# Reordering the first loads, the first basis blocks and four PSUM copies of a graph-network kernel

## The reference, cut to what matters

```python
h = jnp.maximum(_layernorm(x, axis=-1), 0.0)
x = x + _L0_gnn_ref(h, edge_index, Wq, Wk, Wv, bq, bk, bv)
# layer 0: q, k, v = proj(Wq), proj(Wk), proj(Wv); only the last head has scores that are not all zero
masked = jnp.zeros_like(scores).at[-1, src, dst].set(scores[-1, src, dst])
att = jax.nn.softmax(masked, axis=-1)
out = jnp.einsum('hnm,hmd->hnd', att, v)
# layer 1, twice, for r in range(2):
w = jnp.einsum('rb,bio->rio', att, basis)      # 30 matrices of 512 x 512, two sums of them
msg = jnp.where((edge_type == 0)[:, None], msgs[0], msgs[1])
agg = jax.ops.segment_sum(msg, row, num_segments=x.shape[0]) + x @ root + bias
```

## Time and profile before

| what | value |
|---|---|
| median of 3 runs | 642.83 us (642.61 to 643.83) |
| the profiled execution, own time | 641.3 us |
| its span in the trace | 639.5 us |
| TensorE busy | 592.7 us, 93% of the span |
| VectorE busy | 489.5 us, 77% |
| ScalarE busy | 229.5 us, 36% |
| GpSimd busy | 183.9 us, 29% |
| mean DMA rate | 192 GB/s |

### The profile page before, as it was taken

One profiled execution on the slowest core, in us unless ns is written; L12 is line 12 of the kernel. 1 busy time (PEld: TensorE's weight loads), 2 busy tenths in 40 slices (PEclk: granted clock), 3 DMA queues, 4 the chain that ended last, 5 costly groups with the idle time before them and its releaser, 6 DMA issues.

```text
span 639.5 us, 6502 instructions
## 1 busy us (share of the span) xinstructions
PE 592.7 (93%) x2062; PEld 326.1 (51%) x2062; DVE 489.5 (77%) x1054; ACT 229.5 (36%) x455; POOL 183.9 (29%) x229
## 2 busy tenths in 40 slices
PE   4899999998899999999988999997988889999997
PEld 2444445653346644334765786443545445555544
DVE  5489999999999998374747666464687778898266
ACT  2001121510002310206710673310767677785111
POOL 7920000001100000003620372075756556730000
PEclk9899999999998999999999989999989999999999
DMA  8957657669987597700600013475766667740000
GB/s 299 408 198 299 239 191 252 272 237 420 420 333 279 189 377 271 331 1 0 262 3 0 2 38 121 176 216 172 216 184 218 193 208 212 239 142 1 0 16 34
DMA packets 27737, 122.64 MB, mean 192 GB/s; under 512 B 4528, under 2 KB 9392, under 8 KB 22704
## 3 DMA queue, kind: packets, MB, share of 16 engines
q1 hardware_dynamic: 15376, 64.46, 26.9%
q0 software_dynamic: 12320, 57.68, 26.4%
HBM read 120.56 MB, written 1.57 MB: 191 GB/s over the span
## 4 chain that ended last, share of the span: by engine, by line
PE 79%; DVE 10%; DMA 3%; issue 3%; ACT 2%; another core or an unknown queue 2%; POOL 1%; SPq 0%; DVEq 0%
PE ps L1353 25%; PE ps L1696 12%; PE ps L1405 12%; PE ps L1736 8%; PE ps L1589 7%; PE ps L1801 4%; DMA mixm<-basis_p_dram 3%; PE ps L1382 2%; PE ps L1492 2%; DVE node L953 2%; PE ps L1791 2%; DVE mixm L871 2%; DVE node L949 1%; PE ps L1360 1%
## 5 line engine op out<-in xcount | busy, mean ns | idle before, releaser
L871 DVE SCALAR_TENSOR_TENSOR mixm<-mixm,mixc 128x1024 f32<-128x1024 f32 x104 | 126.2, 1285 | 0.0
L1405 PE MATMUL ps<-mixm 128*128 128x512 f32 x240 | 109.9, 604 | 5.8 <-DMA mixm<-basis_p_dram 5.8
L1736 PE MATMUL ps<-m_hi,oh_r 128*128 128x512 f32 x99 | 74.0, 747 | 10.9 <-DVE m_lo L1209 8.2
L1405 PEld LDWEIGHTS ps<-mixm 128*128 128x128 f32 x240 | 45.2, 193 | 57.6 <-issue 47.3
L500 POOL DMA_DIRECT2D mixm<-basis_d_dram x30 | 16.5, 551 | 180.0 <-DVE mixm L871 180.0
L540 POOL DMA_INDIRECT node<-nodes_scratch,idx x54 | 52.3, 968 | 55.3 <-DMA nodes_scratch<-mixm 29.5
L526 POOL TENSOR_TENSOR mats<-mats 128x1152 f32<-128x1152 f32 x10 | 26.2, 2630 | 108.5 <-ACT mats L672 108.4
L754 ACT ACTIVATE m_hi<-node 128x512 fp32r<-128x512 f32 x54 | 33.9, 628 | 53.0 <-issue 22.6
L540 POOL DMA_INDIRECT mixm<-nodes_scratch,idx x45 | 43.6, 970 | 30.0 <-DVE m_lo L1209 15.9
L1696 PE MATMUL ps<-w1b,node 128*128 128x512 f32 x96 | 51.1, 619 | 0.0
L1696 PE MATMUL ps<-w1b,mixm 128*128 128x512 f32 x90 | 45.9, 592 | 0.0
(11 more groups left out here) (238 smaller groups left out, 986.3 us busy)
## 6 DMA issues: line engine op xcount, KB each, us to landing
mixm<-basis_p_dram SPq DMA_DIRECT2D x40, 768.0 KB, 7.0
mixm<-basis_d_dram POOLq DMA_DIRECT2D x30, 1024.0 KB, 7.9
mixm<-ga_w_dram SPq DMA_DIRECT2D x2, 2048.0 KB, 11.5
node<-edge_attr_dram SPq DMA_DIRECT2D x18, 192.0 KB
mixm<-w_hh_dram SPq DMA_DIRECT2D x1, 3072.0 KB, 10.8
mixm<-w_ih_dram SPq DMA_DIRECT2D x1, 3072.0 KB, 10.4
mixm<-edge_attr_dram SPq DMA_DIRECT2D x15, 192.0 KB
node<-roots_dram SPq DMA_DIRECT2D x1, 2048.0 KB, 9.9
```

The lines of the kernel that those rows point to most:

```text
L871: nc.vector.scalar_tensor_tensor(out=acc, in0=basis, scalar=scale, in1=acc, op0=ALU.mult, op1=ALU.add).then_inc(mix_done, 1)
L1405: ins = nc.tensor.matmul(bank[6 + n % 2], spread[:, b // PB, j].rearrange("p r n -> p (r n)"), ring_p[:, b % PS, m * F:(m + 1) * F], start ...
L1736: ins = nc.tensor.matmul(bank[7], oh_w[:, t // 3 % 3, t % 3, :], m[:, t % 3, :], start=m is m_hi and t % LW == 0, stop=m is m_lo and (t % ...
```

## The change

Four things are done. SyncE issues `pairc` first, then the edge lists, block 0 of the basis, `x`, block 1, and only then `wqkv`. TensorE does `mix_rows(0)` and `mix_rows(1)` in front of the transposes and `mix_rows(2)` in front of the q and k projection. In layer 0 ScalarE copies all four chunks of `hT`, and VectorE none. ScalarE copies the middle one of the three chunks of `attT`. The semaphore counts stay what they were.

```diff
         def _(sp):
+            sp.dma_start(pairc[:], a["pairc"]).then_inc(ld_sp, 16)
             sp.dma_start(edge_i[:], a["edge"]).then_inc(ld_edge, 16)
-            sp.dma_start(x[:], a["x"]).then_inc(ld_x, 16)
-            sp.dma_start(pairc[:], a["pairc"]).then_inc(ld_sp, 16)
...
             load_p(0)
+            sp.dma_start(x[:], a["x"]).then_inc(ld_x, 16)
+            load_p(1)
             sp.dma_start(wqkv, a["wqkv"]).then_inc(ld_l0, 16)
             sp.dma_start(bqk[:], a["bqk"]).then_inc(ld_l0, 16)
-            load_p(1)
...
             def hT_act(s):
-                for c in (1, 3):
+                for c in (range(FC) if s == 0 else (1, 3)):
                     act.wait_ge(hT_mm, FC * s + c + 1)
-                    nc.scalar.copy(hT[:, c, :], bank[HB[s][c]][:, 0:N]).then_inc(hT_s, 1)
+                    nc.scalar.copy(hT[:, c, :], bank[HB[s][c]][:, 0:N]).then_inc(hT_s if c % 2 else hT_v, 1)
...
+            act.wait_ge(attT_mm, 2)
+            nc.scalar.copy(attT[:, 1, :], bank[1][:, 0:N]).then_inc(attT_ok, 1)
             act.wait_ge(deg_mm, 1)
...
             def normalised_rows():
-                hT_vec(0)
                 dve.wait_ge(hT_v, 2)
...
-            for j in range(NT):
+            for j in (0, 2):
                 dve.wait_ge(attT_mm, j + 1)
                 nc.vector.tensor_copy(attT[:, j, :], bank[j][:, 0:N]).then_inc(attT_ok, 1)
...
             mix_rows(0)
+            mix_rows(1)
             transpose_h(0, normalised(0))
             pe.wait_ge(out_set, 1)
             strays = pe.value_load(outside_i[0:1, 0:1])
-            mix_rows(1)
+            mix_rows(2)
             pe.wait_ge(hT_v, 2)
             pe.wait_ge(hT_s, 2)
             pe.wait_ge(ld_l0, 32)
             chain(bank[0][:, 0:N], [(wqkv[:, c, 0:2 * D0], hT[:, c, :]) for c in range(FC)]).then_inc(l0_mm, 1)
-            mix_rows(2)
```

## The result

The changed kernel took 637.10 us in the median of 4 runs (635.86 to 638.42) against 643.33 of the kernel before (642.61 to 648.33), a ratio of 0.9882 with a 95% interval of 0.9835 to 0.993. That is 4.5 to 10.6 us, where 3.4 were forecast: the direction was right and the size, in this measurement, about twice too small. The profiled executions differ by much less, 638.42 us against 641.3, with spans of 636.6 and 639.5. A difference of 2.9 us in one pair and 6.2 in the other asked for more timings. Four more were made, each beside runs of the kernel before.

A forecast was written before the change was run, and what follows sets the result against it. The prediction took VectorE's stall behind its branch, for which TensorE waits, to bound the kernel's start. 2.95 + 1.2 + 1.02 + 0.47 - 2.26 = 3.4 us gained takes the median from 642.83 to 639.4 us, range 636.8 to 642.8.

The forecast's parts named there:

- VectorE's gap is a fetch of code: VectorE's 7.68 us stall between its small cast and first hT copy is code fetched after the branch, behind data.
- The gap moves with the branch, 2.26 us lost: x behind block 0 delays VectorE's statistics and branch; the stall keeps 7.68 us and ends at 21.8, losing 2.26 us.
- the rival that I gave 0.10: VectorE's stall ends when it ends now, so 2.26 us are not lost: gain 5.7, time 637.1 us, chance 0.10.
- The waits that go, 2.95 and 1.2 us: VectorE's wait of 2.95 us for TensorE's first count goes wholly; of the next, 2.06 us, 1.2 go.
- 1.02 us by the copies of hT, 0.47 by attT: VectorE without hT copies gains 1.02 us before the one-hots; ScalarE's middle attT copy gains 0.47 us at the softmax.
- TensorE's order: mix_rows(1) before the transposes is hidden by the wait for h; mix_rows(2) precedes the projection; no term in the sum.
- The clock does not fall in the changed kernel: Projection runs at the upper clock; the rival that the clock falls all the same: chance 0.22, gain 2.0, time 640.8 us.
- Nothing is given back behind the softmax: Later block transfers come earlier too; the rival that basis-block waits grow: chance 0.08, time 642.3 us and more.
- The fetch becomes slower: Rival: GpSimd's earlier 1 MB loads lengthen VectorE's stall by as much as 6.1 us; time 645.5 us, chance 0.15 in all.

The follow-up runs named there:

- b1: The kernel before with the two sides of VectorE's branch swapped, the taken side right behind the branch: 647.94 us against 645.43, ratio 1.0051.
- a1: The changed kernel timed again beside the kernel before: 638.06 us against 639.37, ratio 0.9972.
- b3: The changed kernel timed a third time beside the kernel before: 639.05 us against 645.43, ratio 0.9904.
- c3: The kernel before with only SyncE's loads in the new order, a single profiled execution: span 625.8 us, softmax left at 99.35.
- c1: The kernel before, unchanged, profiled once more: span 623.0 us, softmax left at 95.27 us.
- a3: The changed kernel with TensorE's old order of blocks 1 and 2: 635.44 us, ratio 0.9933 to the kernel before.
- d2: Second timing of a3's kernel, beside the changed kernel: 620.04 us against 625.06 of the kernel before, ratio 0.994.
- d4: The kernel before, unchanged, in its fourth profile: softmax left at 95.63 us.
- c4: The kernel before with 12 idle matmuls on TensorE before its wait for VectorE's hT copies: 623.01 us against 623.15, ratio 1.0002.
- b2: Against the kernel before: swapped VectorE branch, new loads, hT copies still shared, attT's middle chunk on ScalarE, block 2 moved later: 645.21 us, ratio 1.001.

## Why the prediction was right or wrong

- **VectorE's gap is a fetch of code.** Right as far as runs can show it. In b1 the gap goes when the taken side stands behind the branch, and another appears at the jump over the other side; instruction packets pass inside both. The rule of the Trainium skill that I named (Runtime: NRT & Kernel Launch, section Instruction fetch mechanics) says that a jump out of the held pages waits for a DMA fetch, and b1 agrees with it.
- **The gap moves with the branch, 2.26 us lost.** This is the step of the sum that failed. `x` did land later, and the statistics began at 8.57 (forecast 8.85). But the gap did not keep its 7.68 us; it shortened to 6.93, and VectorE was back at 20.76, not at 21.8: 1.23 us late where 2.26 were charged. In a1 and b3 it was back at 19.35 and 19.61, and with the loads alone (c3) at 19.20. The gap was 5.99 to 6.93 us in the profiles with the new loads and 6.05 to 7.68 in those with the old. Part of this shows in the instruction packets: the first comes 3.6 to 4.1 us after the cast with the new loads and 3.8 to 4.6 with the old. Why it comes sooner stays open. So the truth lies between my forecast and the rival that I gave 0.10, that the stall ends when it ends now: in the mean the branch moved by 1.5 us and the stall's end by 0.9.
- **The waits that go, 2.95 and 1.2 us.** Right for the profile that was shown: nothing is left of the first, and 0.67 us of 2.06 are left of the second. They are not a constant of the kernel before, though: in c1 the two are 1.28 and 1.95 us, since neither its clock fell nor was its gap as long.
- **1.02 us by the copies of hT, 0.47 by attT.** The latter measured 0.45 (1.16 to 0.71 us of wait). The former is in the one-hots' start: 22.43 against 22.26, so 0.17 late where 1.24 was forecast. The measured terms sum to 2.95 + 1.39 + 0.45 - 0.17 = 4.6 us, and 4.07 arrived at the softmax; the first tiles took 0.45 us each on VectorE instead of 0.39, for a reason that I did not test.
- **TensorE's order.** I charged nothing for it and said that block 1 is hidden by the wait for `h`. Right: a3 and d2 without the new order lose nothing.
- **The clock does not fall in the changed kernel.** Right in all five profiles up to the softmax. Missing was that in the kernel before it falls in two profiles of four only, so that the 1.4 to 1.7 us are not always there to be gained. And where it does not fall over the projection it falls later: by the estimate above the two without the low projection, c1 and d4, lose as much up to 446 us (5.1 and 5.1) as the two with it (4.8 and 5.1). They leave the softmax 2.6 us earlier in the mean, and are 1.3 us ahead at the first matmul of layer 2. In the changed kernel it falls behind the softmax, at the 96 matmuls, in four profiles of five.
- **Nothing is given back behind the softmax.** Right in the mean: at the first matmul of layer 2 the means of the profiles are 267.8 (four before) and 264.5 (five changed), 3.3 us apart, against 3.4 at the softmax. The 1.7 us of the 96 matmuls are made up elsewhere in that stretch; where, was not taken apart.
- **The fetch becomes slower.** It did not. The reading behind this rival was weak: the 13.8 us are the transfers of 1024 KB and the 9.8 us those of 768 KB, so they differ in size and not only in what shares the engines.
- **The number.** 3.4 us was forecast, and the first timing measured 6.2 us between the medians (0.9882). The step that charged the whole 2.26 us is 1.03 us of what was missing. The rest is not in the front; the other timings say less than the first, so scatter is the likely cause, which is argued and not shown. I took the three runs, within 1.2 us of each other, for how well the kernel repeats, and called 1.3 us what can be told from no change; in one set alone it spans 8.6 us. That the front shows just 3.4 in the mean of all profiles is in part luck. My sum was built on the profile of the kernel before with the latest softmax (98.17, where the mean is 96.76), and for that profile and the changed kernel's mean the gain is 4.8 us.

## What to carry to other kernels

Look at what an engine does right behind its branch. The gap does not show in busy time and is named only "issue". It belongs to one engine, so take work that another engine waits for away from that engine around its branch. Turning the branch round only moves the fetch to the jump over the other side; it could pay only where that jump is off the chain, which no run here tried. Size a gain of half a per cent by a milestone in several profiles, such as the first matmul after a stage, because the end of the span carries the scatter of all stages behind it. And follow the gain past the milestone: a low clock that is gone from one stretch can stand in the next, as it did here in c1, d4 and c4.

## What the runs showed of the hardware that I had not expected

- A taken branch cost VectorE 5.99 to 7.7 us while the data queue used 93% of the DMA engines (11 to 20 us, kernel before); the jump over unused code at 80 us, in b1 and b2, cost 4.20 and 4.29 us. TensorE's branch at line 1494 cost nothing that the trace shows.
- The same stage with indirect gathers took 178 us in two sets of runs and 191.5 to 199.1 in the others, while the kernel before took the same time in front of it. One chip number has both.
- The low clock over one 8-matmul projection came in two of four profiles of one kernel, after 2.82 and 2.27 us of idleness, and stayed away after 2.29 and 0.95.
- Up to 446 us the lower clock cost about 5 us, by the estimate above, in all four profiles of the kernel before and in three of the five of the changed one, though it stood at different places.
